# Heads' operands loaded within the projections, shorter shift rows, and the last expert taken tile by tile

## What is computed

```python
Q, K, V = content @ Wq, content @ Wk, content @ Wv       # 16 heads of 16
scores = einsum('bqhd,bkhd->bhqk', Q, K) / sqrt(16)
alpha = softmax(scores)                                    # over all keys
alpha = where(causal, alpha, 0)                            # masked after the softmax
x = layernorm(x + einsum('bhqk,bkhd->bqhd', alpha, V))
...
probs = softmax(h @ router.T); top 2 of 8 experts, capacity 1280
pre, gate = rows @ w1.T, rows @ wg.T                       # 256 -> 1024
y = (pre * silu(gate)) @ w2.T                              # 1024 -> 256
x = layernorm(x + weighted sum of the experts' rows)
```

## Time and profile before

| what | value |
|---|---|
| median of the runs | 1819.73 us |
| the profiled execution | 1823.27 us |
| its span in the trace | 1821.49 us |
| mean granted clock of TensorE | 0.971 of full speed |
| projections, to the first score of attention | 0 to 121.8 us |
| 32 heads of attention | to about 1090 us |
| normalising, routing | to about 1195 us |
| eight experts and the output | to the end |

### The profile page before, as it was taken

The page is one execution under the profiler, slowest core; times in us unless marked ns, Lnnn a source line. Parts: engine busy times, 40 slices in busy tenths (PEclk is TensorE's granted clock), DMA queues, the critical chain, the costliest instruction groups (busy, mean ns, idle before and its releaser), DMA issues. The chain is left out here.

```text
span 1821.5 us, 31571 instructions
## 1 busy us (share of the span) xinstructions
PE 1649.9 (91%) x10818; PEld 1009.3 (55%) x10818; DVE 1170.4 (64%) x2192; ACT 1287.8 (71%) x1485; POOL 302.6 (17%) x296
## 2 busy tenths in 40 slices
PE   7949999999999999999999996479999999999995
PEld 6713333333333333333333332459988998889985
DVE  6847777777777776767786865834444544554474
ACT  7739999999999999999999995423333342432333
POOL 0000000000000000000000001042524425344154
PEclk9969999999999999999999998789999999999998
DMA  5562101010101010101010005222322313323143
GB/s 167 188 160 69 36 18 35 17 35 17 35 17 35 17 35 19 34 20 32 22 31 23 30 0 170 84 70 59 68 57 64 104 15 106 70 58 104 12 127 115
DMA packets 74742, 108.19 MB, mean 59 GB/s; under 512 B 10778, under 2 KB 59715, under 8 KB 74672
## 3 DMA queue, kind: packets, MB, share of 16 engines
q1 hardware_dynamic: 59792, 89.42, 15.6%
q0 software_dynamic: 14880, 17.82, 5.5%
HBM read 75.77 MB, written 35.91 MB: 61 GB/s over the span
## 5 line engine op out<-in xcount | busy, mean ns | idle before, releaser
L690 ACT ACTIVATE probs<-scores 128x1536 f32<-128x1536 f32 (+1 forms) x384 | 520.6, 1379 | 43.1 <-PE scores L620 37.8
L733 DVE TENSOR_REDUCE sums<-expq 128x1 f32<-128x1408 f32 (+6 forms) x448 | 347.5, 828 | 13.1 <-ACT expq L696 13.1
L620 PE MATMUL scores<-aq,ak 98*128 98x512 bf16 (+3 forms) x1280 | 303.6, 352 | 57.6 <-DMA aq<-shift_dram 22.7
L636 PE MATMUL o_ps<-probs,vh 128*32 128x512 f32 (+3 forms) x2560 | 339.0, 541 | 0.0
L1372 ACT ACTIVATE gate<-up_ps 128x512 f32<-128x512 f32 x128 | 76.6, 598 | 315.6 <-PE up_ps L1199 304.7
L620 PE MATMUL scores<-ak,aq 98*128 98x512 bf16 (+3 forms) x1184 | 263.7, 342 | 17.1 <-ACT probs L690 9.0
L696 ACT ACTIVATE expq<-scores 128x1536 f32<-128x1536 f32 x192 | 274.7, 1449 | 1.9
L720 DVE TENSOR_TENSOR hidden<-probs,after 128x384 f32<-128x384 f32 x128 | 70.9, 554 | 239.2 <-ACT probs L690 239.2
L620 PEld LDWEIGHTS scores<-aq,ak 98*128 98x128 bf16 x1280 | 96.5, 98 | 230.7 <-ACT probs L690 73.2
L620 PEld LDWEIGHTS scores<-ak,aq 98*128 98x128 bf16 x1184 | 91.0, 98 | 238.4 <-ACT expq L696 94.7
L1199 PE MATMUL up_ps<-xeT_hi,wup_hi 128*128 128x512 f32 x512 | 201.6, 394 | 7.0 <-DVE mid L1680 3.0
(11 more groups left out here) (237 smaller groups left out, 2570.3 us busy)
## 6 DMA issues: line engine op xcount, KB each, us to landing
raw<-w_T SPq DMA_DIRECT2D x16, 1024.0 KB, 7.8
split_dram<-parts SPq DMA_DIRECT2D x48, 256.0 KB, 2.9
aq<-split_dram SPq DMA_DIRECT2D x192, 64.0 KB
raw<-wg_T SPq DMA_DIRECT2D x8, 1024.0 KB, 5.0
ak<-split_dram SPq DMA_DIRECT2D x32, 192.0 KB
xT<-x_T SPq DMA_DIRECT2D x8, 512.0 KB, 4.8
ak<-split_dram SPq DMA_DIRECT2D x32, 128.0 KB
x_sb<-x_tok SPq DMA_DIRECT2D x1, 4096.0 KB, 25.8
```

Source lines behind the costliest of these rows:

```text
L620: last = nc.tensor.matmul(dst[:, at:at + w], still, moving[0:KS, lo:lo + w], start=True, stop=True, skip_group_check=True)
L636: last = nc.tensor.matmul(dst[32 * r:32 * r + 32, BLK - w:BLK], vh[j % 2][:, k, :], probs[:, m % P_RING, at:at + w], start=first, stop=Tru ...
L690: last = nc.scalar.activation(probs[:, m % P_RING, 0:w], src[:, 0:w], ACT.Exp, scale=HD ** -0.5)
L733: last = nc.vector.tensor_reduce(sums[:, j % 2, col:col + 1], expq[:, n % X_RING, at:at + w], AX.X, ALU.add)
```

## The change

1. **Start.** The order of loads is weight, x, weight, weight, x. Each weight has its own semaphore, and TensorE waits for the one it needs.
2. **Shift rows.** Only the bf16 part of the bound is kept (`shift[:, b, :]`). The second row is a row of zeros, stored once at the start. The bound of batch 0 is written by VectorE in one pass. For batch 1 VectorE makes only the maxima and `k8`, an eighth of the largest key norm, and goes on to the flag; ScalarE writes the rows, the last 512 columns straight from `norm`, whose copy is left out. ScalarE issues their store in the fallback's block.
3. **Operands of heads 0 and 1** are loaded within the projections: queries of head 0 ahead of the stores of block 4, its keys and shift rows ahead of block 5's, head 1's likewise with blocks 6 and 7. To this end `attn`, `aq`, `ak`, `qn`, `shift` lie beside `v_all`, the rows of -4 are written by GpSimd at the start, and SyncE waits at block 4 for the stores of batch 0. The wait for the last stores moves to the fallback's block.
4. **Attention.** TensorE waits for the fills and for V at its fourth score tile, ScalarE for the fills and `head_done` at its second.
5. **Last expert.** The scale for token tiles and the first six row tiles becomes one (`BEFORE`, 38 columns), made between the products of the second pass. VectorE takes four token tiles in eight and GpSimd two; ScalarE takes the six row tiles between its gates. The last four tiles come tile by tile out of the down products (`down_last`, four PSUM banks) and are measured, scaled and normalised by VectorE alone, in two pairs.

```diff
@@ projections, SyncE
+                load_w(0)
+                load_x(0)
+                load_w(1)
+                load_w(2)
+                load_x(1)
+                sp.wait_ge(none_ready, 1)
+                for b in range(B):
+                    sp.dma_start(shift_dram[1, b * H:(b + 1) * H, :], none[:]).then_inc(none_stored, 16)
...
+                    if n == NG:
+                        for k in range(NG):
+                            sp.wait_ge(parts_stored[k], 16 * 6)
+                        sp.wait_ge(none_stored, 16 * B)
+                        sp.wait_ge(shift_stored[0], 16)
+                    if n >= NG:
+                        j = (n - NG) // 2
+                        if n % 2 == 0:
+                            load_queries(sp, j, j, a_loaded[j])
+                        else:
+                            load_keys(sp, j, j, a_loaded[j])
+                            load_shifts(sp, j, j, a_loaded[j])
@@ projections, ScalarE, behind the last block
+                act.wait_ge(norm_read, 3 * NB + 3 - 1)
+                act.wait_ge(k8_ready, 1)
+                for cols, of in ((slice(0, N - BLK), qn[:, 0:N - BLK]), (slice(N - BLK, N), norm[0:H, 0, :])):
+                    nc.scalar.activation(shift[:, 1, cols], of, ACT.Identity, bias=k8[:], scale=0.125).then_inc(shift_ready, 1)
@@ projections, VectorE
-                    nc.vector.tensor_scalar(bound[:], qn[:], kmax[:], 0.125, ALU.add, ALU.mult).then_inc(dve1, 1)
...
-                    nc.vector.tensor_copy(shift[:, 0, b * N:(b + 1) * N], bound[:]).then_inc(dve1, 1)
-                    dve.wait_ge(dve1, step + 5)
-                    nc.vector.tensor_tensor(shift[:, 1, b * N:(b + 1) * N], bound[:], shift[:, 0, b * N:(b + 1) * N],
-                                            ALU.subtract).then_inc(shift_ready, 1)
+                bound_batch(0)
+                nc.vector.tensor_scalar(shift[:, 0, :], qn[:], kmax[:], 0.125, ALU.add, ALU.mult).then_inc(shift_ready, 1)
...
+                bound_batch(1)
+                nc.vector.tensor_scalar(k8[:], kmax[:], 0.125, None, ALU.mult).then_inc(k8_ready, 1)
@@ fallback's block
+                for n in range(NG):
+                    sp.wait_ge(parts_stored[n], 16 * 6 * B)
                 with sp.If(loose > 0):
...
+            @block.scalar
+            def _(act):
+                act.wait_ge(shift_ready, 1 + 2)
+                act.dma_start(shift_dram[0, H:NH, :], shift[:, 1, :]).then_inc(shift_stored[1], 16)
@@ attention
-                for j in range(2):
-                    load_head(j, j)
...
-                    pe.wait_ge(vh_ready, i * 2 + (j + 1))
                     for t in range(NS):
                         fill(i, j, t)
+                        if t == 3:
+                            pe.wait_ge(fills_ready, 9)
+                            pe.wait_ge(vh_ready, i * 2 + (j + 1))
@@ experts
-        BY_ACT, BY_DVE, BY_POOL = 2, 3, 3
+        BY_ACT, BY_DVE, BY_POOL = 2, 4, 2
+        LAST_TILES = ((0, 1), (2, 3))
...
+                        if g == 1 and not prep:
+                            for t in range(NA):
+                                for f in range(FC):
+                                    if t == 0:
+                                        pe.wait_ge(mid_split, count(2 * FC, i, j, g * FC + f + 3))
+                                    last = down_last(f, t)
+                                last.then_inc(y_ready, 1)
+                            return
...
+                            if g == 1 and not prep and f == 1:
+                                root(0, BEFORE)
+                                act.wait_ge(scale_ready, 1)
+                            if g == 1 and not prep and f >= 2:
+                                for normalise, t in of_act[2 * (f - 2):2 * (f - 1)]:
+                                    normalise(t)
...
+                            if g == 1 and not prep and f == 0:
+                                variances()
+                            if g == 1 and not prep and f == 1:
+                                scales()
+                            if g == 1 and not prep and f >= 2:
+                                for t in of_dve[4 * (f - 2):4 * (f - 1)]:
+                                    token(t)
...
+                def last_tiles(n, tiles):
+                    for t in tiles:
+                        dve.wait_ge(y_ready, 2 * E - 1 + t + 1)
+                        leave(LASTJ, NA + t, last_ps[t], False).then_inc(y_done, 1)
+                        measure_row(NA + t, t + 1)
...
+                    for t in tiles:
+                        at = nc.vector.bn_aggr(agg[:, t, :], fstats[:, Y_AT[NA + t], :])
+                    link7(at)
+                    nc.vector.tensor_scalar(fvar[:, of], agg[:, tiles[0]:tiles[-1] + 1, 1], LN_EPS, None, ALU.add).then_inc(var2_ready, 1)
+                    dve.wait_ge(std2_ready, n + 2)
+                    link7(inverse_root(nc, link7, fvar[:, of], fstd[:, of], frstd[:, of], ftmp[:, of]))
```

More of the change, by code:

```diff
@@ L840, in program @@
         with ExitStack() as st, nc.Block() as block:
+            assert nc.sbuf_base == v_at and 2 * CT * D <= NH * NT * HD
+            xin = [sb(st, f"xin{j}", [P, CT, D]) for j in range(2)]
             raw2 = sb(st, "raw2", [P, FC, D])
@@ L1201, in up, with down_last @@
                     return last
+                def down_last(f, t):
+                    for a, b in PAIRS:
+                        last = nc.tensor.matmul(last_ps[t], mid2[a][:, f, t * P:(t + 1) * P], w2[b][:, f, :],
+                                                start=(f == 0 and (a, b) == PAIRS[0]), stop=(f == FC - 1 and (a, b) == PAIRS[-1]))
+                    return last
                 def down(f, nt):
@@ L1674, in body @@
                             dve.sem_inc(c_done, 1)
+                            if not prep:
+                                for t in [*range(NA), *range(2 * NA, CT)]:
+                                    measure_row(t, 0)
                         for f in range(FC + 1):
@@ L1689, in body @@
                                 measure_tokens(range(LD // 2 * (f - FC + 1), LD // 2 * (f - FC + 2)))
-                            if g == 1 and not prep and 1 <= f <= FC // 2:
-                                for n in range(3 * (f - 1), 3 * f):
-                                    token(of_dve[n])
+                            if g == 1 and not prep and f == 0:
[5 more added lines that the diff above has]
+                                    token(t)
                         if g == 0:
```

247 lines of the change are left out of this document (131 added, 116 removed).

## The result

| | before | after |
|---|---|---|
| median of the runs, us | 1819.78 (1819.26 to 1819.84, 4 runs) | 1795.88 (1795.19 to 1797.05, 4 runs) |
| profiled execution, us (span) | 1823.27 (1821.5) | 1795.19 (1793.4) |

The kernel is 23.9 us faster, ratio 0.987 with a 95% interval of 0.9858 to 0.9882. Forecast were 1785.4 us and a range of 1782.5 to 1793.5. The sign is right, the size is not: 34.3 us were forecast, and even the slow end of the range is passed by 2.4 us.

What follows compares the result with a forecast made beforehand. TensorE, 91% busy, was taken as idle mainly at four seams: start, batch boundary, handover, last expert. Their 2.5 + 5.0 + 19.9 + 6.9 = 34.3 us, off the median 1819.73, gave 1785.4; range 1782.5 to 1793.5.

Steps and rivals of the forecast that it cites:

- In the 32 heads of attention and in eight experts the change touches almost nothing: Attention heads and eight experts: no gain or loss, so only the four seams were summed.
- so nobody waits for these: Projections, blocks 4 to 7: stores queued behind the moved operand loads delay nobody; cost 0, bounds 0 and 1.0.
- Start: First loads: x's first block ahead of two weights lets TensorE begin at 8.2; 2.5 us gained, bounds 1.0 and 3.5.
- Batch boundary: Between the projections' batches: 3.6 from fewer VectorE passes, 1.5 from no clock dip; 5.0 us gained, bounds 3.5 and 5.4.
- copy intervals all near 9.5: Sign of being right, projections: VectorE's copy intervals all near 9.5, with no half clock at the boundary.
- Handover: Projections to attention: first score at 101.9 against 121.81; 19.9 us gained, bounds 15 and 20.6.
- rival A: Projections to attention only half won, a new wait replacing the loads: 6 lost, 1791.4 us; chance 0.12.
- Last expert: Last expert and output: regrouped scales, down products tile by tile, earlier scatters; 6.9 us gained, bounds 3 and 7.5.
- B: Last expert: VectorE and ScalarE fall behind, output tiles land late; 1.5 gained in place of 6.9, 1790.8 us; chance 0.07.
- D: Attention: new waits in each of 32 heads make the kernel slower, 1827 at 1.3 us a head; chance 0.04.
- C: Last expert: ScalarE's table load takes the skill page's 2.7 us, not 1.28; sum 33.0, 1786.7 us; chance 0.01.
- E: Boundary between batches: only 3.5 gained and no clock gain, 1786.9 us; within the forecast, no chance of its own.

Runs made afterwards that it cites:

- e1: Kernel before with an unused tile of 32 bytes a partition ahead of the routing's tiles: 1827.21 us against 1820.23, ratio 1.0037.
- e2: Kernel after with `agg` allocated behind the routing's tiles: 1789.22 us against 1820.23 for before, ratio 0.9828.
- e12: Kernel after with `agg` behind the routing's tiles, run again unchanged in another set: 1795.29 us, ratio 0.9842 to before.
- e6: Kernel after with `agg` behind, operand loads of heads 0 and 1 issued at the start of attention again: 1805.93 us against 1795.29.
- e7: Kernel after with `agg` behind, first five loads again in the order w, w, w, x, x: 1798.48 us against 1795.29.
- e8: Kernel after with `agg` behind, three more VectorE passes over 16 x 2048 at the batch boundary: 1800.42 us against 1795.29.
- e4: Kernel before with only the change's experts' part, `agg` behind the routing's tiles: 1813.96 us against 1820.23, ratio 0.9963.
- e14: Kernel before with only the change's experts' part, `agg` behind, run again unchanged in another set: 1820.75 us, ratio 0.9986.
- e5: Kernel before with 32 unused bytes ahead of the very first tile, so weights and `xeT` both move: 1828.27 us against 1823.32.
- e13: Kernel after, run again unchanged in another set: 1802.78 us, ratio 0.9888 to before.

## Why the prediction was wrong

**The step that failed** is not a term of the sum but the sentence that there is nothing to sum: "In the 32 heads of attention and in eight experts the change touches almost nothing". For the heads it held (966.3 against 966.5). For the experts it cost 7.0 us in e1 and 6.7 in e2, the larger part of the 10.5 by which the median was missed. The diff had the line, and the change part passed over it. Nothing in the trace of before could have priced it, but one operand of 1536 matmuls on the path moved, and that a step of 227 ns might not survive this deserved a bound. Without it the result lies within the stated range of 1782.5 to 1793.5: e2's ratios, taken from before's 1819.73, give 1788.4 in the first set and 1791.0 in e12's. Whether it meets the forecast's own range, to 1789.5, depends on the set. My worse bounds all at once, 1798.2, would have held the 1795.88; the stated range left them out.

**The second step that failed** is "so nobody waits for these", with the cost of 0 for the operand loads: the handover waits for the stores of the last block, and with the loads ahead of them they land 2.7 us later, 5.2 behind their issue where e6 without these loads has 2.5 (below).

**Start.** 2.5 forecast, bounds 1.0 to 3.5; 3.2 in the runs of e7, 3.9 in its stretch and 3.5 on average over all traces. TensorE began at 7.57, not 8.2, since the 768 KB of w and x landed by 5.47 and not by 6.08, and nothing of it "goes back": the second block of x was in time.

**Batch boundary.** 5.0 forecast, 6.4 between the two executions. e8 gives the mechanism and its price: 5.5 for 3.9 us of passes, as its expectation of 5.4 said. The wait was sized right (3.6 forecast, 3.5 measured), the clock was not: 1.5 forecast, 3.0 in before. It is not the same in every execution: in e1, whose half clock lasts 3.4 and not 6.8, the stretch is 42.9 and not 44.2. The sign "copy intervals all near 9.5" did not come: they are 10.63, 8.83, 8.83 and 9.50, as VectorE, behind by its pass, catches up while TensorE never stops.

**Operand loads at no cost.** Right for the projections' blocks (37.8 from the fourth to the eighth norms, with them in after and without them in e6), and e6 shows what it is worth to have them there. Wrong for what comes behind: see the handover.

**Handover.** 19.9 forecast, 16.7 measured from the eighth norms, or 17.3 with the copy of 0.6. "Land 2.9 later" was sized from the trace of before, where even the last of the stores took only 2.5. In after SyncE's queue had issued the last of six at 88.35, and the third block begins at 94.10, with this wait ahead of it (waits of SyncE, 85 to 96):

```profile
SPq L534 <- DMA split_dram<-parts: 3.0, 1, 3.0
```

The wait ends at 93.6: 5.2 behind the issue of the last store, 2.3 more than I put. In e6, without the operand loads among the stores, it ends 2.5 behind. ScalarE wrote its rows at 87.01 to 89.15 about as forecast, so the stores were the bound, not the rows. That is rival A, in a small size (2.6 of its 6 us), and from a cause that it did not name: the stores land late behind the loads that the change put in front of them.

**Last expert.** 6.9 forecast, 6.3 in e4 (2.7 in e14). In after it is 5.4, as its own 192 up matmuls also take 6.2 ns more, 1.2 us. The three claims hold: six statistics of 2.06 stand where the chain of 3.37 stood; the last pair of tiles leaves VectorE at 1783.6; the last scatter starts 74.7 us behind the expert's first gate, where it was 80.1. One did not: "GpSimd may scatter once the token output has landed, some 1794". The first scatter, which waits for it, starts 62.9 us behind that gate, 1796.5 on the old clock where I had 1794.5. So the ten scatters still go nearly back to back from 1773.83, and VectorE's last pair is ready 0.8 before GpSimd takes it up. The bound is shared, not VectorE's alone.

**Rivals.** B (the end not won) falls with e4, and D (heads longer) with the table. C: the loads of ScalarE's table take 1.28 in after too, at 1752.89 for one, and the way to the square root and back takes 3.2 in all (1751.17 to 1754.33) with the root of 0.24 in it. The Trainium skill, ScalarE: Activation LUTs, section "Table sets: the hidden batching unit", has some 2.7 for each switch, a load and what goes with it; two of them do not fit into 3.2, so the trace does not agree with the page. E does not occur.

**The base.** I took the gain between profiled executions off the median. That was right in form; but before's profiled execution holds a stall of some 3 us in a place where after's has none, so the two spans differ by 28.1 where the medians differ by 23.9.

The fastest kernel that ran is e2_agg_behind, the change with `agg` allocated behind: 1789.2 us, 31.0 below before (28.1 in the set of e12) and 6.7 below the change as it was made.

## What to carry to other kernels

A new tile, however small, moves every tile that is allocated behind it, and a matmul's step can depend on how its two operands lie to each other: put additions at the end, or compare the addresses of the operands of the hot loop, and look at its period before anything else when a gain comes out short. Cut both traces at the same events and subtract; the stretch that nobody changed is the first to look at. And when transfers are moved into a queue, ask not only whether the queue has room but whether anybody waits for what stands behind them: the landing time of a store, read in the old kernel, did not hold behind the new loads.

## What the runs showed of the hardware

- 128 x 512 matmuls in fp32r, back to back at full clock: 227 ns a step with both operands at the same place modulo 512 bytes (before, e2, e5), 233 with 32 bytes between them (after, e1). 128 x 256: 120.0 and 116.6, the other way round. For `y_ps`, 117.1 with 64 bytes and 120.5 with 96.
- A stop of 3.9 us of VectorE at the batch boundary cost 5.5 (e8), as TensorE was then granted 0.54 of its clock from 61 to 64, half speed for most of it.
- The last of six 256 KB stores landed 2.5 us behind the end of its issue (before, e6), and 5.2 (after) where loads of keys and shift rows had been issued ahead of the six.
- One and the same kernel differed by 6.1 to 6.9 us between sets of executions (e2 and e12, after and e13, e4 and e14; the experiments' sets ran on different chips), where before differed by 3.2 to 3.7: what a change gains can depend on the set even when each repeats to within about 0.2%.
